# Window attention with split operands in the mixing of the heads, on one Trainium2 core

## The reference

```
xw  = rolled x cut into windows                       # (b*nw, 49, 192)
qkv = xw @ qkv_w.T + qkv_b ;  q, k, v = split heads
attn = softmax(q*16**-0.5 @ k.T + bias + shift mask)  # per head 49 x 49
out = (attn @ v) heads side by side                   # (b*nw, 49, 192)
out = out @ proj_w.T + proj_b                         # "mixing of the heads"
x   = x + rolled back out
```

## Time and profile before

| | |
|---|---|
| median of three runs | 4775.11 us |
| the profiled execution's own time | 4771.51 us |
| its span, first to last instruction | 4769.7 us |
| PE busy | 4464.8 us (94%) |
| DVE busy | 4038.5 us (85%) |
| ACT busy | 2472.6 us (52%) |
| POOL busy | 2481.5 us (52%) |
| mean granted TensorE clock | 0.989 of full speed |

### The profile page before, as it was taken

How to read it: one execution, slowest core, us unless ns; L and a number is a source line. 1 busy time by engine, 2 the same in 40 slices (tenths; PEclk the granted TensorE clock), 3 DMA queues, 4 the chain that set the end, 5 groups by cost and what they waited for, 6 DMA issues and landing times. The chain is left out here.

```text
span 4769.7 us, 140614 instructions
## 1 busy us (share of the span) xinstructions
PE 4464.8 (94%) x51720; PEld 3768.6 (79%) x51720; DVE 4038.5 (85%) x7594; ACT 2472.6 (52%) x4850; POOL 2481.5 (52%) x2098
## 2 busy tenths in 40 slices
PE   0599999999999999999969999999999999999999
PEld 0488888888888888888857777777777777777777
DVE  6788888888888888888838888888888888888887
ACT  0244444444444444444416666666666666666665
POOL 1245555455545555455525555555555555555555
PEclk9999999999999999999969999999999999999999
DMA  8011111111111111111112222222222222222222
GB/s 341 21 38 38 39 39 41 37 39 39 41 37 38 39 39 40 37 39 39 37 40 66 71 67 70 67 70 68 68 71 66 71 67 70 69 68 70 67 71 59
DMA packets 389802, 286.01 MB, mean 60 GB/s; under 512 B 147164, under 2 KB 388044, under 8 KB 388556
## 3 DMA queue, kind: packets, MB, share of 16 engines
q1 hardware_dynamic: 387012, 283.15, 20.3%
q10 hardware_dynamic: 2736, 2.14, 0.1%
HBM read 120.34 MB, written 87.31 MB: 44 GB/s over the span
## 5 line engine op out<-in xcount | busy, mean ns | idle before, releaser
L887 POOL TENSOR_TENSOR E<-E,ri 128x588 f32<-128x588 f32 x512 | 601.5, 1175 | 410.4 <-DVE ri L1119 410.4
L893 POOL TENSOR_TENSOR L<-L,mx 128x294 f32<-128x294 f32 x512 | 483.4, 944 | 511.7 <-DVE mx L1105 511.7
L603 PE MATMUL ps_o<-w,g_hi 128*128 128x384 f32 x2352 | 710.6, 365 | 5.9 <-DVE g_lo L543 4.1
L415 ACT ACTIVATE gF<-ps_g,b1f 128x512 f32<-128x512 f32 x588 | 406.0, 691 | 394.0 <-PE ps_g L634 391.3
L976 ACT ACTIVATE PT<-ps_t 98x588 f32<-98x588 f32 x512 | 342.7, 669 | 461.4 <-PE ps_t L1253 451.3
L1101 DVE SCALAR_TENSOR_TENSOR L<-ps_s,bias 128x588 f32<-128x588 f32 x512 | 384.1, 750 | 230.8 <-PE ps_s L1170 230.8
L603 PE MATMUL ps_o<-w,g_lo 128*128 128x192 f32 x2352 | 534.9, 255 | 0.0
L1170 PE MATMUL ps_s<-Kp,Q 32*64 32x98 f32 x12288 | 494.0, 259 | 1.5 <-POOL E L887 0.6
L442 POOL TENSOR_TENSOR res<-xt,b2b 128x768 f32<-128x768 f32 x98 | 181.1, 1848 | 591.4 <-DVE x L491 591.4
L401 ACT ACTIVATE h_hi<-ps_h,hbias 128x512 fp32r<-128x512 f32 x196 | 123.2, 679 | 703.1 <-PE ps_h L618 703.1
L603 PEld LDWEIGHTS ps_o<-w,g_hi 128*128 128x128 f32 x2352 | 429.7, 189 | 27.1 <-issue 25.1
(11 more groups left out here) (211 smaller groups left out, 12030.9 us busy)
## 6 DMA issues: line engine op xcount, KB each, us to landing
xs<-in_x SPq DMA_DIRECT2D x8, 4704.0 KB, 22.5
xt<-in_x SPq DMA_DIRECT2D x98, 384.0 KB, 3.4
x_cells<-x SPq DMA_DIRECT2D x784, 48.0 KB
xb<-x_cells SPq DMA_DIRECT2D x128, 294.0 KB
Vx<-V SPq DMA_DIRECT2D x512, 73.5 KB
out<-yo SPq DMA_DIRECT2D x128, 294.0 KB
Kp<-K SPq DMA_DIRECT2D x256, 98.0 KB, 2.0
Kp<-K SPq DMA_DIRECT2D x256, 49.0 KB, 2.2
```

The source lines that it names most:

```text
L415: act.activation(gF[f % 4][:, :], ps_g[:, f % 2, :], ACT.Gelu, bias=b1f[:, f:f + 1]).then_inc(s_gelu, 1)
L603: last = pe.matmul(dst, g[:, f, P * k:P * (k + 1)], w, start=(f == 0 and i == 0), stop=(f == FT - 1 and i == 1))
L887: pool.tensor_tensor(e, e, ri[p][:, :].unsqueeze(2).to_broadcast([P, HEADS, T]), ALU.mult)\
L893: pool.tensor_tensor(l, l, mx[p][:, HS:HEADS].unsqueeze(2).to_broadcast([P, HEADS - HS, T]), ALU.subtract).then_inc(s_sbp, 1)
```

## The change

Six things change together, all in the attention:

1. The mixing uses split operands: `wp` is split into `wproj_*`, ACT writes `o_hi` where it wrote `oT`, and a new DVE step `heads_lower`, two instructions per quarter, writes the remainders `o_lo` and the upper half of `o_hi[:, 1]`. `mix` issues 10 fp32r matmuls instead of 4 fp32 ones, and waits for `s_o`, which DVE now signals.
2. POOL subtracts all twelve heads' maxima; DVE's L1109 is gone.
3. `values(1)` moves from quarter 3 of the slot before into quarter 0 of the unit's own slot; `values(0)` moves from the end of quarter 2 to quarter 3.
4. `mix(0)` and its `finish` move from quarter 2 to quarter 1, `turn` behind PV of quarter 0, `project(0)` behind PV of quarter 1, `project(1)` ahead of PV of quarter 2.
5. On DVE the sums of the exponentials come before `lower`.
6. SP spreads the values (now of unit u) ahead of the keys (of unit u+1).

```diff
-            TURN, KEYS, OUT0, QRY, VAL, OUT1 = 0, 2, 4, 5, 6, 8
+            VAL1, TURN, OUT0, KEYS, QRY, VAL0, OUT1 = 0, 1, 3, 4, 6, 7, 8
...
@@ block.sync, slot
+                    if is_unit(u):
+
+                        for half in range(2):
+                            sp.wait_ge(s_vc[half], u + 1)
+                        for w in range(2):
+                            for e in range(2):
+                                sp.dma_start(Vx[c][T * e:T * (e + 1), w:NW:2, JP * HD * e:JP * HD * (e + 1)],
...
                     if is_unit(u + 1):
...
                                 sp.dma_start(Kp[d][rows, k, e, :, :], K[rows, k, :, :]).then_inc(s_kp[d], 16)
 
-                        for half in range(2):
-                            sp.wait_ge(s_vc[half], u + 2)
...
@@ block.gpsimd, less_max
-                    l = L[p][:, HS:HEADS, :]
-                    pool.tensor_tensor(l, l, mx[p][:, HS:HEADS].unsqueeze(2).to_broadcast([P, HEADS - HS, T]),
-                                       ALU.subtract).then_inc(s_sbp, 1)
+                    l = L[p][:, :, :]
+                    pool.tensor_tensor(l, l, mx[p][:, :].unsqueeze(2).to_broadcast([P, HEADS, T]),
+                                       ALU.subtract).then_inc(s_sub, 1)
@@ block.scalar, slot
+                        if is_unit(u) and p == 0:
+                            act.wait_ge(s_v, 2 * u + 2)
+                            act.activation(V[0:T2, 2:4, :], v_sum(1), ACT.Copy).then_inc(s_vc[1], 1)
...
+                        if is_unit(lu):
+                            act.wait_ge(s_pv, k + 1)
+                            upto(act, s_pj, 2 * (lu - 1))
+                            act.wait_ge(s_vb, lu + 1)
+                            for h, rows in enumerate((P, CB)):
+                                last = act.activation(o_hi[lc][lp][0:rows, h, :], ps_v[0:rows, h * T2:(h + 1) * T2],
+                                                      ACT.Identity, bias=vb[lc][0:rows, h:h + 1])
+                            last.then_inc(s_oh, 1)
                         if nxt:
                             if p == 0:
                                 upper(i, c, 0)
                                 upper(i, c, 1)
@@ block.vector
+                def heads_lower(u, c, p):
+                    dve.wait_ge(s_oh, UP * u + p + 1)
+                    dve.scalar_tensor_tensor(out=o_lo[c][p][:, :], in0=ps_v[:, 0:T2], scalar=vb[c][:, 0:1],
+                                             in1=o_hi[c][p][:, 0, :], op0=ALU.add, op1=ALU.subtract)
+                    dve.scalar_tensor_tensor(out=o_hi[c][p][CB:P, 1, :], in0=ps_v[0:CB, T2:2 * T2],
+                                             scalar=vb[c][0:CB, 1:2], in1=o_hi[c][p][0:CB, 1, :],
+                                             op0=ALU.add, op1=ALU.subtract).then_inc(s_o, 1)
...
+                        if is_unit(u - 1):
+                            heads_lower(u - 1, 1 - c, p)
                         if is_unit(u):
                             dve.wait_ge(s_sc, k + 1)
...
-                            l = L[p][:, 0:HS, :]
-                            dve.tensor_tensor(l, l, mx[p][:, 0:HS].unsqueeze(2).to_broadcast([P, HS, T]),
-                                              ALU.subtract).then_inc(s_sub, 1)
-                        if is_unit(u - 1) and p == 2:
+                        if is_unit(u - 1) and p == 1:
                             finish(i, c, 0)
@@ block.tensor, mix and slot
                     pe.wait_ge(s_o, UP * v + 2 * half + 2)
                     if is_unit(v + 2):
                         if half == 0:
-                            pe.wait_ge(s_xl, 2 * (v + 2) + 2)
+                            pe.wait_ge(s_vc[1], v + 2)
                         else:
-                            pe.wait_ge(s_qkm, 3 * (v + 2) + 3)
+                            pe.wait_ge(s_qkm, 3 * (v + 2) + 2)
...
-                        for k in range(2):
-                            last = pe.matmul(ps_w(OUT1 if half else OUT0)[0:T2, C * a:C * (a + 1)],
-                                             oT[d][p][:, k, :], wp[:, k, :], start=(k == 0), stop=(k == 1))
+                        terms = W_P.terms(o_hi[d][p], o_lo[d][p], slice(0, C))
+                        for k, (w, o) in enumerate(terms):
+                            last = pe.matmul(ps_w(OUT1 if half else OUT0)[0:T2, C * a:C * (a + 1)], o, w,
+                                             start=(k == 0), stop=(k == len(terms) - 1))
...
+                            upto(pe, s_yo, 2 * (u - 1))
```

More of the change, by code:

```diff
@@ L724, in build @@
             PT = [sb(f"PT{b}", [P, JP, T2]) for b in range(2)]
-            oT = [[sb(f"oT{b}{p}", [P, 2, T2]) for p in range(UP)] for b in range(2)]
+            o_hi = [[sb(f"o_hi{b}{p}", [P, 2, T2], f32r) for p in range(UP)] for b in range(2)]
+            o_lo = [[sb(f"o_lo{b}{p}", [P, T2], f32r) for p in range(UP)] for b in range(2)]
             ps_s = ps("ps_s", [P, 2, 512])
@@ L747, in v_sum @@
             def v_sum(half):
-                return ps_w(VAL + half)[0:T2, 0:2 * C].rearrange("p (a c) -> p a c", a=2)
+                return ps_w(VAL1 if half else VAL0)[0:T2, 0:2 * C].rearrange("p (a c) -> p a c", a=2)
             def copied(engine, i, c):
@@ L775, in build @@
             LOADS = 1 + 1
[L776 removed]
+            WEIGHT_LOADS3 = 4
             K_SPREADS = 2 * HB
@@ L869, in _ @@
                 pool.memset(Q[0][:, :, :, :], 0.0)
[L870 to L874, removed]
+                pool.memset(Kp[0][:, :, :, :, :], 0.0).then_inc(s_pad, 1)
                 pool.wait_ge(s_w3, 16 * WEIGHT_LOADS3)
                 pool.wait_ge(s_ws3, 1)
-                for t in range(2):
-                    last = pool.tensor_tensor(W_QKV.parts[2 * t + 1][:, :], raw[:, t, :], W_QKV.parts[2 * t][:, :],
-                                              ALU.subtract)
+                for full, parts in ((raw, W_QKV), (wp, W_P)):
+                    for t in range(2):
+                        last = pool.tensor_tensor(parts.parts[2 * t + 1][:, :], full[:, t, :], parts.parts[2 * t][:, :],
+                                                  ALU.subtract)
                 last.then_inc(s_pad, 1)
@@ L922, in _ @@
                 act.wait_ge(s_w3, 16 * WEIGHT_LOADS3)
-                for t in range(2):
-                    last = act.activation(W_QKV.parts[2 * t][:, :], raw[:, t, :], ACT.Copy)
+                for full, parts in ((raw, W_QKV), (wp, W_P)):
+                    for t in range(2):
+                        last = act.activation(parts.parts[2 * t][:, :], full[:, t, :], ACT.Copy)
                 last.then_inc(s_ws3, 1)
@@ L990, in slot @@
                                 queries_b(i, c)
[L991 to L1006, removed]
+                            if p == 2:
+                                evacuated(i, c, 2)
                 units(act, slot)
@@ L1195, in project, with values @@
                     last.then_inc(s_qk, 1)
-                def values(i, c, half):
-                    v = 2 * i + c + 1
-                    if half == 0:
-                        pe.wait_ge(s_qkm, 3 * v + 2)
-                    else:
-                        upto(pe, s_yo, 2 * (v - 2) + 1)
+                def values(half):
                     for a in range(2):
@@ L1206, in values @@
                         for k, (w, x) in enumerate(terms):
-                            last = pe.matmul(ps_w(VAL + half)[0:T2, C * a:C * (a + 1)], x, w,
+                            last = pe.matmul(ps_w(VAL1 if half else VAL0)[0:T2, C * a:C * (a + 1)], x, w,
                                              start=(k == 0), stop=(k == len(terms) - 1))
```

66 lines of the change are left out of this document (31 added, 35 removed).

## The result

The changed kernel takes 4789.94 us, the median of 20 runs (4777.34 to 4811.18), against 4774.11 for the kernel before in the 20 runs beside it (4772.03 to 4776.53). The ratio is 1.0035, 95% interval 1.0025 to 1.0046: slower by 0.35%. The forecast of 4767 us was 7 us better than before, the result is 16 us worse. The profiled execution took 4791.91 us, with a span of 4790.1.

A forecast was written before the change was run, and what follows sets the result against it. PE's own work plus its waits bounds the kernel: 16.25 + 1.27 = 17.52 us a unit against 17.58, 0.06 x 128 = 8 us off, giving 4767 us. Own range 4745 to 4790; 8 in 10, 4720 to 4820.

The forecast's parts named there:

- PE's work: PE's work per unit without waits: 16.83 - 2.94 + 2.16 + 0.20 = 16.25 us, ten mixing matmuls at 1.08.
- The bound of 1.47: Upper bound in us for one block of split mixing on PE, the old mixing's time; 1.08 was taken.
- The 195 us given for matmuls at the old price: Case of split matmuls costing what an fp32 record does: unit 19.0 us, 195 us slower, 2 in a hundred.
- The wait that comes: PE waits 1.27 us before mix(0) in quarter 1 for DVE's heads_lower, behind lower, upper and turn; replaces 0.75.
- the line between the two rows: DVE time of a 98-element heads_lower instruction, 0.32 us, from rows of 12 elements (0.23) and 392 (0.62).
- Rival 2: Faster: hand-overs overlap more, PE's wait before mix(0) about 0.9 us, unit 17.15, time 4720 us; chance 17%.
- the walk: Chain from turn's end through ACT's upper and DVE's lower and heads_lower to PE's start at 2.57 us.
- What else moves: Other engines' changes stay hidden: POOL's subtraction 1.18 us instead of 0.94, DVE less work, keys 0.6 to 1.4 us spare.
- Rival 3: Slower: keys land 1.5 us later than summed, or finish misses its 0.07 us; unit about 17.8, 4803 us; chance 13%.
- The unit: One unit on PE, work plus wait: 17.52 us against 17.58 before; wrong if not within 17.3 to 17.7.
- the granted clock 1.00 in steady stretches: Sign expected in the changed profile: PE's clock stays full in the steady attention stretch.
- rival 1: Slower: clock falls in PE's longer wait, 1.7 us lost per fall, one unit in eight, 4794 us; chance 25%.

The follow-up runs named there:

- heads first: Changed kernel with DVE's heads_lower of quarter 1 moved ahead of lower in quarter 0; 4615.33 us, ratio 0.9662 to the kernel before.
- filler: Changed kernel with twelve matmuls whose result nobody reads in PE's wait before mix(0); 4748.38 us, ratio 0.9948 to the kernel before.
- half filler: Changed kernel with six matmuls whose result nobody reads in PE's wait before mix(0); 4748.0 us, ratio 0.9957 to the kernel before.
- longer wait: Kernel before with one more DVE reduction, some 0.5 us, ahead of lower, so that project(0) waits longer; 4891.67 us, ratio 1.0256.

## Why the prediction was wrong

**PE's work: right.** 16.25 us a unit forecast, 16.18 measured where nothing waits (heads first). The ten matmuls took 1.07 for 1.08. The bound of 1.47 was far off, the row of the same shape the right one. The 195 us given for matmuls at the old price are against the forecast's 17.52; against the kernel before the same sum gives (19.04 - 17.58) x 128 = 187.

**The wait that comes: right in place, cause and size.** 1.23 us for 1.27 in the unit shown, and 17.35 - 16.18 = 1.17 on average, released by DVE's `o_hi`, behind `lower`, `upper` and `turn`. `heads_lower` took 0.32 and 0.31, the value of the line between the two rows. The Trainium skill (VectorE: DVE Perf Modes, The TRN2 errata) gives 0.26 for an addition of that size, an estimate from its formula; the rows of this place show 0.31 to 0.32, so here the measurement decides. Rival 2, a short wait, did not occur: the walk had no slack, as argued. One small miss of the walk cost nothing: ACT began its copy 0.27 us behind PV (3514.04 against 3513.77), not 0.14, and `upper` still came within 0.03 of the forecast.

**What else moves: right.** The subtraction took 1173 ns, and none of PE's waits is for it. The keys' issue ended at 3525.25, 14.5 us behind the scores at 3510.75, where the sum of the prediction gives 14.6, and PE showed a wait on them only once, of 0.3 us, in 2560 to 4700. Rival 3 did not occur in the changed kernel. It did where the unit became shorter: this is the cap that the prediction named, and heads first ran into it (three waits, 5.2 us in all, and the falls behind them).

**The unit: right.** 17.41 in the unit shown and 17.35 on average for 17.52, inside the 17.3 to 17.7, near its lower end.

**The step that failed: "the granted clock 1.00 in steady stretches".** The forecast took the time as 128 units at full clock and gave rival 1, the falling clock, 25%. That rival is what happened. The prediction had seen the place ("In front of the wait stand PE's lightest works"), and then took the milder side. Its evidence against, a wait of 0.75 us in each unit at full clock, says nothing of longer waits; two unlike rows, this one and the start of the attention, were all there was, and 1.27 is well past the one shown harmless. Filler and half filler show the clock to be the whole of the difference between 4748 and 4790, and the longer wait in the kernel before shows 1.09 us to be enough there.

**Rival 1's own terms.** A share of one unit in eight was put forward; measured were 20 short falls in some 120 units, one in six. A fall was priced at 1.7 us, all the PE work lost in 3.4 us at half rate; it costs 1.2 (filler), 1.4 (mean of the units with a fall) or 1.3 (longer wait). A reason that fits is that PE's next wait is for DVE, which does not slow down, so part of the delay is absorbed; that was not tried by itself. The long stretch at half rate, 19 us, was in no case of the prediction. That rival 1's own 4794 lies near the 4790 found is partly luck: the clock cost 42 to 46 us and not its 27, and the unit was 0.17 us shorter than forecast, 22 us in all. With both put right, 4767 - 22 + 46 = 4791.

The Trainium skill (TensorE: Matmul & The Clock Gate, Part 1) has the gate go to half rate after an idle stretch and stay warm otherwise; the same part also tells of a kernel in which short idle times between groups of matmuls make the clock go up and down, which rival 1 left out. The rows contradict the first as it was read into rival 1 and agree with the second: the clock fell behind waits of 1.2 us with PE busy 2.85 of 4 us. That it stayed at 0.50 with PE busy 10.00 of 10 fits neither.

## What to carry to other kernels

Work out each new wait as here, but when a wait of PE grows past the longest that the trace shows at full clock, price the clock with it and give that case the greater chance. On an engine that works in order, look at what is ready while it idles: two instructions that PE waits for stood behind two that it did not need yet. Before giving up a change that does not pay, take its one bad wait away: here the six edits cost 16 us with it and gained 158 without (176 with the values spread ahead of the load).

## What the runs showed of the hardware

- TensorE can stay at half rate while it is busy all the time. From 3358.5 to 3413.1 the granted clock was 0.50, with PE busy 10.00 of 10 us in the slice from 3400 to 3410. In heads first it was 0.50 over 2630 to 2640, PE busy all the time too. Such work is transposes of 64x64, scores tiles of 32x64 and PV of 32 columns among the projections. What ended these stretches, and why most falls last 3.4 us and these longer, stays open.
- Twenty runs of one kernel spread over 34 us (4777 to 4811), where kernels whose clock does not fall spread over 3 (filler, 4747.11 to 4749.93) to 13. The mean clock differs from run to run, 0.970 to 0.980; a single run would have shown anything from equal to 0.8% slower.
- A single late transfer can be enough. In heads first the parameters' issue on SP lasted 1.59 us instead of 0.51, PE waited 2.22 us for the keys, and 13.7 us at half rate followed; so they did behind a wait of 1.92. But in the kernel with plain fp32 mixing one wait of 1.77 us for the keys brought no fall.
- Two short waits were not one long one. The split mixing alone has two waits in each unit, 0.68 and 0.41 us, 1.6 us apart, and a clock of 1.00; the longer wait in the kernel before has the same 1.09 us in one piece, and 45 falls in the same 2000 us. The mixing differs too, so the reason stays open.
- A GpSimd operation can hold up one of VectorE. The same subtraction of 128x294 on VectorE takes 0.47 us beside POOL's own half of the subtraction; it takes 1.24 us when 0.91 of them fall beside POOL's residual (split mixing alone), and 1.87 when 1.55 do. Both times it ends 0.32 to 0.33 us behind the residual. VectorE's steps that read PSUM are not stretched: in the changed kernel `heads_lower` and the bias step beside a residual take their usual 0.32, 0.31 and 0.77.
